# A graph layer on one core: the last tiles are finished an iteration sooner, and the picks are made at the end of a quarter

## The chip, the core and the metric

One NeuronCore of a Trainium2 chip runs the whole kernel as one launch. The time is the device time of one execution in microseconds (us). Before the change it is 906.05 us, the median of three runs (905.99 to 906.22).

## The reference

A layer of message passing over 6250 nodes with 128 features, and 106250 edges sorted by their target. Cut to what matters:

```python
src = x[edge_src]
parts = [relu(x)]
for t in range(3):                       # edge types
    msg = relu(src @ W_e[t].T + b_e[t])
    msg = where(edge_type == t, msg, 0)
    parts.append(segment_sum(msg, edge_dst, 6250))
agg = concatenate(parts, axis=1)         # 6250 x 512
for t in range(3):                       # node types
    updated = where(node_type == t, agg @ W_n[t].T + b_n[t], updated)
out = layernorm(x + (updated + x))
```

All values are fp32. The last 6250 of the edges before sorting are self loops, one for each node.

## The kernel before, in words

**Setup.** TensorE makes a table of all messages (node by edge type, 18750 rows of 128) in device memory. VectorE meanwhile splits the edges into kinds. The last 9050 edges are *early* edges: their source rows are gathered during setup, 36 pairs of chunks. Self loops are taken straight from the table. Up to 128 edges of each of 90 rows, those whose source is among the last 1280 nodes, are *dense*: their source row is picked by a product with a one-hot. What is left of the first 97200 edges is *main*.

**Main stage.** There are 45 iterations j (`NI`) of four quarters g (`NG`), and the code numbers the quarters q = 4j + g. Quarters 0 and 2 hold three chunks of 128 edges, quarters 1 and 3 four. GpSimd gathers a chunk's message rows with one indirect DMA (L753), 14 in an iteration, 630 in all. TensorE sums a group: message rows times a one-hot of their targets (`sum_group`, L1652). GpSimd's gathers for (j+1, g) wait for the sum (j, g) only. VectorE makes the one-hots an iteration ahead (`one_hot`, L1252) and adds the sums into `acc` (L1264) one or two quarters after the iteration's end (`add_sums`).

Around each sum the engines take more steps, each by its own fixed list (`quarter` in each engine's block). TensorE, VectorE, ScalarE and SP wait for each other by semaphores alone, and each runs its list in order. The steps, by where a planner function puts them:

- *Pairs of dense rows* r: `turn_at(r)` is 4r + 3 up to pair 36 and three quarters more for each later one, so 147, 150, 153, ... 171. At that quarter TensorE turns the pair (`dense_turn`, L1673, 20 matmuls), a quarter later VectorE masks it (L1338), three quarters later TensorE makes its messages (`dense_make`, L1686 and L1690), after four it sums them (`dense_sum`, L1698), after five VectorE adds them (`dense_add`). The turn reads one-hots, the *picks* (`dense_onehot`, L1328, two instructions), that VectorE makes at `pick_at(r)`, one quarter after the turn of pair r-1. The picks wait for that turn, since it reads the same tile.
- *Early pairs* go in the same way up to pair 35, with `early_turn`, `early_make` (L1626, L1631), `early_sum`, `early_add`.
- *Tiles* of 128 nodes. Tile t is turned on TensorE at quarter 4(t + 3) (`finish_turn`, L1736). A quarter later its self-loop rows are transposed (`place_selfs`, L1713); after two VectorE adds `acc` and these into a stage (`finish_acc`, L1399); after four TensorE multiplies by the node weights (`finish_linear`, L1747 to L1755); after five VectorE takes the sum with 2x and its statistics (`finish_h`, L1367 to L1375); after six ScalarE takes a root (L917); after seven VectorE writes the row (`finish_y`). The turn of a tile waits for `finish_acc` of the tile before, whose bank it writes; the product waits for `finish_h` of the product before in the same bank, an extra tile's included.
- *Extra tiles*, the last four (45 to 48), whose sums are ready sooner: turned at quarters 69, 97, 133 and 152, multiplied (`LINEAR_AT`) at 74, 102, 138 and 154, their `finish_h` a quarter later.

**Last iteration** (`last_iteration`): tiles 0 to 40 are done in the loop; tiles 41, 42, 43 (sets 2, 0 and 3 of the tiles' buffers) and 44 are finished here. Tiles 42, 43 and 44 have their products behind the last group's sum, 43 and 44 after all additions.

SP loads and stores by its own list: the pairs' rows and types two iterations ahead, tiles in batches of four, stores of finished tiles at the end.

Of the kernel before, what the change touches and what calls it, by code (L numbers as in the profile page):

```python
# [30 lines left out]
ALU = mybir.AluOpType  # L31
# [93 lines left out]
assert sum(n for _, n in BATCHES) == NA and BATCHES[-1] == (SPLIT, TAKEN_LATE)  # L125
# [26 lines left out]
def pick_at(r):  # L152
    return turn_at(r - 1) + 1 if r else NG // 2
# [19 lines left out]

LIMIT_STEP = 15
# [12 lines left out]
LINEAR_AT = [next(q for q in range(at + 2, at + 6) if q % NG == 2) for at in EXTRA_AT]  # L187
# [7 lines left out]


def tile_step(q, later):
    t = (q - later) // NG - (LATE - 1)
    return t if (q - later) % NG == 0 and 0 <= t < SPLIT else None
# [32 lines left out]
def build(nc, x, src, dst, etype, ntype, w_e, b_e, w_n, b_n, out):  # L232
# [6 lines left out]
    with ExitStack() as ctx:  # L239
# [154 lines left out]
        iota_moved = sem("iota_moved")  # L394
        hot_iota_set, acc_zeroed, limits_set = sem("hot_iota_set"), sem("acc_zeroed"), sem("limits_set")
# [101 lines left out]
        def _(sp):  # L497
# [168 lines left out]
            for tile, tiles in BATCHES:  # L666
                if NI <= tile + tiles + LATE and tile + tiles <= SPLIT:
                    sp.wait_ge(fin_y[0], tile + tiles)
                    store_fin(tile, tiles)
            sp.wait_ge(fin_y[2], 1)  # L670
            store_fin(SPLIT)
            sp.wait_ge(fin_y[0], Z0_TILES)
            store_fin(SPLIT + 1)
            sp.wait_ge(ctl_set, 1)
            need = sp.value_load(ctl[0:1, 0:1], min_val=0, max_val=1)
            store_extra(KE)
            sp.wait_ge(fin_y[3], 1)
            store_fin(NA - 1)
            sp.wait_ge(stored[0], 16 * STORES)
# [33 lines left out]
        def _(pool):  # L713
# [13 lines left out]
                      allow_small_or_imprecise_dtypes=True)  # L727
# [54 lines left out]
        def _(act):  # L782
# [136 lines left out]
            def quarter(j, g):  # L919
# [13 lines left out]
                if g == 2 and j > 1:  # L933
                    mask_selfs(j - 2)
# [5 lines left out]
            def last_iteration():  # L940
                finish_x(0, 2, first=True)
                mask_selfs(SPLIT + 1)
                mask_selfs(SPLIT + 2)
                mask_selfs(ORDER[KE])
                finish_x(Z0_TILES - 1)
# [4 lines left out]
                finish_sd(Z0_TILES - 1)  # L950
# [22 lines left out]
        def _(dve):  # L973
# [389 lines left out]
            def finish_h(tile, nth, z=0, slot=None):  # L1363

                x_tile = xg[:, at(tile if slot is None else slot), :].rearrange("p a d -> p (a d)")
                dve.wait_ge(fin_xt[z], nth + 1)
                fin_link(dve.tensor_tensor(h[z][:, :], x_tile, x_tile, ALU.add), nth, z, 1)  # L1367
# [35 lines left out]
            def quarter(j, g, bases_of, pair_base):  # L1403
# [3 lines left out]
                if q in PICKS:  # L1407
                    dense_onehot(PICKS[q])
# [29 lines left out]
                if tile_step(q, ACC_LATER) is not None:  # L1438
# [100 lines left out]
        def _(pe):  # L1539
# [227 lines left out]
            def quarter(j, g):  # L1767
# [12 lines left out]
                if t is not None:  # L1780
                    place_selfs(t, t)
# [100 lines left out]
```

## Time and profile before

| what | value |
|---|---|
| median of three runs | 906.05 us |
| the profiled execution | 907.5 us |
| its span, first to last instruction | 905.7 us |
| busy: TensorE matmul, weight load | 716.2, 598.9 us |
| busy: VectorE, ScalarE, GpSimd | 616.4, 145.0, 673.7 us |
| mean granted TensorE clock | 0.912 of full |

The trace is of one execution. It gives each instruction's start, length, line and tile, the idle time before it, and what ended that idle time. Tiles share memory, so one name can stand for another: `order_f` is the masked pair, `first_wide` and `dense_f` are picks, `work` the one-hots, `emsg` the early masks or the stage of set 2, `src_wide` the dense rows' nodes. "issue" as a releaser means that the profile shows nothing that was waited for.

### The profile page before, as it was taken

Reading aid. Unit: us, or ns where it says so; the run is one execution under the profiler, and the core shown is the slowest. Engines: PE = TensorE matmul, PEld = TensorE weight load, DVE = VectorE, ACT = ScalarE, POOL = GpSimd, SP = SyncE. Lnnn points to the kernel's source line nnn. Section 1 sums busy time; section 2 is a strip of 40 time slices with the busy share of each in tenths; the row PEclk is TensorE's granted clock in tenths of the full one; section 3 lists DMA queues with packets and bytes.
Section 4 is the critical chain, followed back from the end, with each engine's and each line's share of the span. In section 5 each row is a group of like instructions: output and inputs, shape, how many; then the busy total and the mean of one; then the engine's idle time right before and its main releaser. Section 6 shows DMA issues by size and latency. Waiting matters only on the chain.

```text
span 905.7 us, 14050 instructions
## 1 busy us (share of the span) xinstructions
PE 716.2 (79%) x4555; PEld 598.9 (66%) x4555; DVE 616.4 (68%) x1468; ACT 145.0 (16%) x397; POOL 673.7 (74%) x719
## 2 busy tenths in 40 slices
PE   5593056887997988888898878989888798769786
PEld 3362056776876876676687766878767587658674
DVE  7999988476676557557575754775675477656656
ACT  3393000111111101111110120110112011001120
POOL 7777777777777777777777777777777777777772
PEclk9796569998999989999999998999899999989989
DMA  8595533433443343343344342434435334324321
GB/s 245 161 311 147 136 97 76 113 97 50 146 117 105 97 110 107 103 111 92 94 118 116 96 115 78 121 107 111 106 96 114 93 85 118 102 63 128 97 53 45
DMA packets 72065, 101.39 MB, mean 112 GB/s; under 512 B 18137, under 2 KB 55517, under 8 KB 71995
## 3 DMA queue, kind: packets, MB, share of 16 engines
q0 software_dynamic: 22432, 45.99, 21.3%
q1 hardware_dynamic: 46861, 50.45, 18.5%
q10 hardware_dynamic: 2702, 4.08, 1.5%
q8 instruction: 37, 0.61, 0.3%
q14 instruction: 33, 0.27, 0.1%
HBM read 87.47 MB, written 12.97 MB: 111 GB/s over the span
## 4 chain that ended last, share of the span: by engine, by line
POOL 44%; PE 18%; issue 16%; DVE 15%; DMA 6%; SPq 0%; DVEq 0%; POOLq 0%; ACT 0%; ACTq 0%
POOL tab L753 44%; DMA tab<-message_table,idx_t 5%; PE ps L1652 5%; PE ps L1755 3%; PE ps L1673 3%; DVE src_wide L1098 1%; DVE stage L1131 1%; PE ps L1690 1%; PE ps L1686 1%; DVE first_wide L1034 1%; PE ps L1748 1%; DMA dst_raw<-in_dst 1%; PE ps L1631 1%; DVE dst_raw L1091 1%; PE ps L1698 1%
## 5 line engine op out<-in xcount | busy, mean ns | idle before, releaser
L753 POOL DMA_INDIRECT tab<-message_table,idx_t x630 | 595.2, 945 | 194.1 <-issue 185.6
L1652 PE MATMUL ps<-work,tab 128*128 128x126 f32 x1260 | 180.4, 286 | 94.0 <-DMA tab<-message_table,idx_t 68.7
L1252 DVE TENSOR_TENSOR work<-key_t,ps 128x378 f32<-128x378 f32 (+1 forms) x180 | 108.8, 606 | 208.3 <-PE ps L1652 203.7
L1652 PEld LDWEIGHTS ps<-work,tab 128*128 128x128 f32 x1260 | 163.6, 199 | 106.2 <-issue 68.4
L1264 DVE TENSOR_TENSOR acc<-ps,acc 128x126 f32 (+1 forms) x306 | 96.2, 314 | 30.0 <-DVE acc L1264 9.9
L1755 PE MATMUL ps<-wn_t,stage 128*128 128x384 f32 x282 | 104.8, 512 | 0.0
L749 POOL DMA_INDIRECT xg<-in_x,esrc_t x67 | 72.4, 1081 | 20.7 <-issue 16.8
L1755 PEld LDWEIGHTS ps<-wn_t,stage 128*128 128x128 f32 x282 | 56.3, 200 | 40.4 <-issue 5.6
L1673 PE MATMUL ps<-first_wide,tab 128*128 128x128 f32 x450 | 62.8, 291 | 9.5 <-DVE first_wide L1328 6.5
L1673 PEld LDWEIGHTS ps<-first_wide,tab 128*128 128x128 f32 x450 | 58.9, 207 | 9.9 <-issue 9.9
L896 ACT ACTIVATE stage<-ps 128x128 f32<-128x128 f32 x47 | 12.9, 277 | 297.0 <-PE ps L1755 282.1
L1673 PE MATMUL ps<-dense_f,tab 128*128 128x128 f32 x450 | 60.0, 283 | 0.0
L1673 PEld LDWEIGHTS ps<-dense_f,tab 128*128 128x128 f32 x450 | 56.6, 200 | 0.0
L1370 DVE SCALAR_TENSOR_TENSOR h<-ps,mask,h 128x128 f32<-128x128 f32 x147 | 51.6, 351 | 6.7 <-PE ps L1755 1.5
L1626 PE MATMUL ps<-we_t,emsg 128*128 128x128 f32 x216 | 36.3, 312 | 23.0 <-issue 20.4
L917 ACT ACTIVATE sd<-mv,eps 128x1 f32<-128x1 f32 x49 | 14.3, 294 | 230.2 <-DVE mv L1375 230.2
L1626 PEld LDWEIGHTS ps<-we_t,emsg 128*128 128x128 f32 x216 | 32.0, 220 | 27.0 <-issue 23.8
L1686 PE MATMUL ps<-we_t,order_f 128*128 128x128 f32 x270 | 44.1, 308 | 6.5 <-DVE acc L1264 6.5
L1573 PE MATMUL ps<-we_t,work 128*128 128x384 f32 x98 | 44.5, 540 | 3.3 <-DVEq L995 3.2
L1686 PEld LDWEIGHTS ps<-we_t,order_f 128*128 128x128 f32 x270 | 40.7, 225 | 8.1 <-issue 7.8
L1690 PE MATMUL ps<-we_t,order_f 128*128 128x128 f32 x270 | 44.2, 302 | 0.0
L1338 DVE TENSOR_TENSOR order_f<-ps,dst_raw 128x768 f32<-128x768 f32 x45 | 42.7, 949 | 0.1
(260 smaller groups left out, 1021.4 us busy)
## 6 DMA issues: line engine op xcount, KB each, us to landing
tab<-message_table,idx_t POOLq DMA_INDIRECT x630, 2.6
message_table<-tab SPq DMA_DIRECT2D x24, 384.0 KB, 3.5
dst_raw<-dense_types SPq DMA_DIRECT2D x45, 192.0 KB
wn_raw<-message_table SPq DMA_DIRECT2D x22, 384.0 KB, 3.4
src_wide<-dense_lists SPq DMA_DIRECT2D x45, 128.0 KB, 3.2
we_raw<-early_types SPq DMA_DIRECT2D x18, 192.0 KB
be_b<-early_types SPq DMA_DIRECT2D x18, 192.0 KB
work<-in_x ACTq DMA_DIRECT2D x10, 256.0 KB, 5.0
```

The source lines that it names most:

```text
L749: pool.indirect_dma_start(xg[:, q, :], None, x, bass.IndirectOffsetOnAxis(ap=rows, axis=0)).then_inc(x_gathered, 16)
L753: pool.indirect_dma_start(msg[:, slot, :], None, table, bass.IndirectOffsetOnAxis(ap=rows, axis=0)).then_inc(signal, 16)
L1252: dve.tensor_tensor(hot[:, first:first + n, :].rearrange("p c (t w) -> p c t w", w=WIN), keys.broadcast_to((P, n, T, WIN)), iota_win.rearr ...
L1264: dve.tensor_tensor(cols, sums.rearrange("p (t c) -> p t c", t=T), cols, ALU.add).then_inc(added, 1)
L1370: fin_link(dve.scalar_tensor_tensor(h[z][:, :], lin_bank(z, nth)[:, t * D:(t + 1) * D], mask[:, t, at(tile)], h[z][:, :], ALU.mult, ALU.ad ...
L1573: pe.matmul(ps[:, MSG_PS + i, 0:T * D], xt[:, par, i, :], we_t[:, :], start=True, stop=False)
L1626: pe.matmul(early_made[:, 0, :], exm[:, 0, t, :], we_t[:, t * D:(t + 1) * D], start=(t == 0), stop=False)
L1652: ins = pe.matmul(sums_bank(j, g), msg[:, column, :], hot[:, column, :], start=(c == 0), stop=(c == n - 1))
L1673: ins = pe.matmul(dxt_ps[:, :, s * DENSE:(s + 1) * DENSE], dx[:, (SETS - 1 - s) * DT + k, :], donehot[s][:, k, :, :], start=(k == 0), stop ...
L1686: pe.matmul(dmsg_ps[:, 0, :], dxm[:, 0, t, :], we_t[:, t * D:(t + 1) * D], start=(t == 0), stop=False)
L1690: ins = pe.matmul(dmsg_ps[:, 1, :], dxm[:, 1, t, :], we_t[:, t * D:(t + 1) * D], start=False, stop=(t == T - 1))
L1755: ins = pe.matmul(lin, stage[z][:, i, :], wn_t[:, i, :], start=False, stop=(i == T))
```

## The change

1. **Tiles.** A table `TILE_AT` replaces 4(t + 3). Tiles 0 to 32 keep their quarters (12 to 140). Tiles 33 to 36 are turned at 143, 146, 150 and 153, tile 37 at 156, and from there four quarters apart up to tile 41 at 172; before they were at 144, 148, 152, 156 and 160, up to tile 40 at 172. All steps of a tile keep their distance from its turn. In TensorE's quarter the product now stands ahead of the transposes of the self rows.
2. **Extra tiles.** The last product moves from quarter 154 to 156; tile 36's product is at quarter 157.
3. **Picks** move from the start of VectorE's quarter after a pair's turn to the end of the quarter of that turn.
4. **Last iteration.** It finishes tiles 42, 43 and 44 only. Tile 43 has its stage added behind two groups of the last iteration, not behind all additions, and its product ahead of the last group's sum. Only three type products of tile 44 stand behind that sum.
5. **Checks for the general path.** One GpSimd `affine_select` with a wait sets the limit of the last row, so that tile 43 may be finished early.

```diff
-TAKEN_LATE, LATE = 3, 4
+TAKEN_LATE, LATE = 2, 4
 SPLIT = NA - TAKEN_LATE
-Z0_TILES = SPLIT + 1
-STORES = len(BATCHES) - 1 + TAKEN_LATE
+Z0_TILES = SPLIT
+STORES = len(BATCHES) - 1 + BATCHES[-1][1]
...
 def pick_at(r):
-    return turn_at(r - 1) + 1 if r else NG // 2
+    return turn_at(r - 1) if r else NG // 2
...
+def tile_turns():
+    at = []
+    for t in range(SPLIT):
+        if t < LEAD_FROM - LATE + 1:
+            at.append(NG * (t + LATE - 1))
+        else:
+            at.append(max(NG * (t + LATE - 2), turn_at(t + 1) + ADD_LATER - ACC_LATER, at[-1] + NG - 1))
+    return at
...
-LINEAR_AT = [next(q for q in range(at + 2, at + 6) if q % NG == 2) for at in EXTRA_AT]
+LINEAR_AT = [next(q for q in range(at + 2, at + 8)
+                  if (q % NG == 2 or q >= NG * LEAD_FROM) and tile_step(q, LINEAR_LATER) is None
+                  and tile_step(q - 1, LINEAR_LATER) is None) for at in EXTRA_AT]
...
             pool.iota(limit[:, :], pattern=[[P // 2, 2]], base=-P, channel_multiplier=P // 2,
-                      allow_small_or_imprecise_dtypes=True)
+                      allow_small_or_imprecise_dtypes=True).then_inc(limit_made, 1)
+            pool.wait_ge(limit_made, 1)
+            pool.affine_select(out=limit[:, :], in_=limit[:, :], compare_op=ALU.not_equal, fill=float(NA * P),
+                               base=-(HR - 1), pattern=[[0, 2]], channel_multiplier=1)
...
# VectorE, quarter
                 one_hot(j + 1, g)
-                if q in PICKS:
-                    dense_onehot(PICKS[q])
...
+                if q in PICKS:
+                    dense_onehot(PICKS[q])
                 return pair_base
...
# VectorE, last iteration
-                finish_h(SPLIT - 1, SPLIT - 1)
-                dve.wait_ge(group_summed, NG * j + 3)
                 add_sums(j, 0, bases_of[0])
                 add_sums(j, 1, bases_of[1])
-                finish_acc(SPLIT + 1, Z0_TILES - 1, 0, ADDED["main", j, 1])
+                finish_acc(NA - 1, 0, 3, ADDED["main", j, 1])
+                finish_h(SPLIT - 1, SPLIT - 1)
                 finish_h(SPLIT, 0, 2)
+                finish_y(SPLIT - 1, SPLIT - 1)
+                dve.wait_ge(group_summed, NG * j + 3)
                 add_sums(j, 2, bases_of[2])
-                finish_y(SPLIT - 1, SPLIT - 1)
                 finish_y(SPLIT, 0, 2)
+                finish_h(NA - 1, 0, 3)
                 dve.wait_ge(group_summed, NG * j + 4)
                 add_sums(j, 3, bases_of[3])
                 finish_acc(ORDER[KE], KE, 1, ALL_ADDS)
-                finish_acc(NA - 1, 0, 3, ALL_ADDS)
-                finish_h(SPLIT + 1, Z0_TILES - 1)
+                finish_y(NA - 1, 0, 3)
                 finish_h(ORDER[KE], KE, 1, slot=SLOT_OF[KE])
-                finish_y(SPLIT + 1, Z0_TILES - 1)
-                finish_h(NA - 1, 0, 3)
                 finish_y(ORDER[KE], KE, 1, slot=SLOT_OF[KE])
-                finish_y(NA - 1, 0, 3)
...
# TensorE, last iteration
                 finish_linear(SPLIT - 1)
                 sum_group(j, 1)
-                finish_linear(0, 2, first=True)
-                pe.wait_ge(stage_acc[2], 1)
-                finish_turn(SPLIT + 1, Z0_TILES - 1, len(BATCHES))
                 pe.wait_ge(added, ADDED["dense", j, SIDES - 1])
                 finish_turn(NA - 1, 0, len(BATCHES), 3, first=True)
                 pe.wait_ge(fin_var[1], KE)
                 finish_turn(ORDER[KE], KE, NZ, 1)
+                place_selfs(NA - 1, 0, 3)
+                place_selfs(ORDER[KE], KE, 1)
+                finish_linear(0, 2, first=True)
                 pe.wait_ge(added, ADDED["main", j - 1, NG - 1])
                 sum_group(j, 2)
-                place_selfs(SPLIT + 1, Z0_TILES - 1)
-                place_selfs(NA - 1, 0, 3)
-                place_selfs(ORDER[KE], KE, 1)
+                finish_linear(0, 3, first=True)
                 pe.wait_ge(hot_ready, NG * NI)
                 pe.wait_ge(d_hot, NI)
+                linear_open(KE, 1)
                 pe.wait_ge(added, ADDED["main", j, 1])
-                linear_open(KE, 1)
                 sum_group(j, 3)
-                finish_linear(Z0_TILES - 1)
                 linear_types(KE, 1)
-                finish_linear(0, 3, first=True)
```

The masks of the self rows on ScalarE (`mask_selfs`) and SP's stores follow the tiles in the same way.

## Rows read from the trace of the kernel before

**Rows 1.** The page, part 4: the chain that ended last, by engine.

```profile
POOL 44%; PE 18%; issue 16%; DVE 15%; DMA 6%; SPq 0%; DVEq 0%; POOLq 0%; ACT 0%; ACTq 0%
```

**Rows 2.** One line's instructions: count, shortest/median/longest ns, first and last start.

```profile
L753 POOL DMA_INDIRECT tab<-message_table,idx_t x630: 938/944/1047, 101.5 to 889.5; - x158
```

**Rows 3.** Waits of GpSimd: for whom, us in total, times, longest.

```profile
POOL tab L753 <- PE ps L1652: 8.4, 21, 1.1
```

**Rows 4.** Timeline (start, length, engine, line, count, [idle before]): GpSimd, quarters 157 and 158.

```profile
805.58 0.94 POOL L753 DMA_INDIRECT tab<-message_table,idx_t  x1 [0.85 <-PE ps L1652]
...
810.57 0.94 POOL L753 DMA_INDIRECT tab<-message_table,idx_t  x1 [0.30 <-issue]
```

**Rows 5.** Timeline, quarters 145 to 147, TensorE and VectorE.

```profile
750.27 0.91 PE L1626 MATMUL ps<-we_t,emsg 128*128 128x128 f32 x6
...
752.58 0.18 DVE L1375 BATCH_NORM_AGGREGATE mv<-bnst 128x2 f32<-128x6 f32 x1
...
753.11 1.06 PE L1652 MATMUL ps<-work,tab 128*128 128x126 f32 x8
...
754.24 0.55 DVE L1399 TENSOR_TENSOR stage<-acc,ps 128x384 f32<-128x384 f32 x1
```

**Rows 6.** Timeline, VectorE in quarter 157.

```profile
805.35 0.68 DVE L1252 TENSOR_TENSOR work<-key_t,ps 128x504 f32<-128x504 f32 x1 [7.49 <-PE ps L1652]
...
805.94 0.81 DVE L1328 TENSOR_TENSOR first_wide<-src_wide,ps 128x640 f32<-128x640 f32 x1
...
807.41 0.95 DVE L1338 TENSOR_TENSOR order_f<-ps,dst_raw 128x768 f32<-128x768 f32 x1
...
808.89 0.28 DVE L1367 TENSOR_TENSOR h<-xg 128x128 f32<-128x128 f32 x1
...
810.76 0.18 DVE L1375 BATCH_NORM_AGGREGATE mv<-bnst 128x2 f32<-128x6 f32 x1
```

**Rows 7.** Timeline, TensorE in quarters 159 to 163.

```profile
812.89 1.62 PE L1686 MATMUL ps<-we_t,order_f 128*128 128x128 f32 x6 [4.96 <-DVE acc L1264]
...
819.75 0.33 PE L1747 MATMUL ps<-bn_parts,pick_parts 128*128 128x384 bf16 x1
...
822.49 0.90 PE L1698 MATMUL ps<-first_wide,dense_f 128*128 128x216 f32 x4
...
823.22 1.05 PE L1652 MATMUL ps<-work,tab 128*128 128x126 f32 x8
...
824.11 0.49 PE L1713 MATMUL ps<-ident,wn_raw 128*128 128x128 f32 x3
...
824.44 0.83 PE L1652 MATMUL ps<-work,tab 128*128 128x126 f32 x6
...
826.06 0.91 PE L1686 MATMUL ps<-we_t,order_f 128*128 128x128 f32 x6 [0.79 <-DVE acc L1264]
...
827.88 1.28 PE L1673 MATMUL ps<-first_wide,tab 128*128 128x128 f32 x10
...
830.11 1.05 PE L1652 MATMUL ps<-work,tab 128*128 128x126 f32 x8
```

**Rows 8.** Timeline, TensorE in quarters 153 and 156.

```profile
782.77 2.09 PE L1673 MATMUL ps<-first_wide,tab 128*128 128x128 f32 x10 [2.96 <-DVE stage L1399]
...
795.84 0.32 PE L1747 MATMUL ps<-bn_parts,pick_parts 128*128 128x384 bf16 x1 [3.17 <-DVE mv L1375]
...
800.27 0.83 PE L1686 MATMUL ps<-we_t,order_f 128*128 128x128 f32 x6
```

**Rows 9.** Windows: length, PE, PEld, DVE, ACT, POOL busy, clock, DMA, GB/s.

```profile
797.00:800.00 3.00, 3.00 (x6) 1.69 (x5) 0.86 (x2) 0.00 (x0) 2.13 (x3) 0.50 0.18 45
```

**Rows 10.** Timeline of the last iteration, TensorE and VectorE.

```profile
883.36 1.13 PE L1652 MATMUL ps<-work,tab 128*128 128x126 f32 x8 [0.24 <-DMA tab<-message_table,idx_t]
...
892.19 0.49 PE L1652 MATMUL ps<-work,tab 128*128 128x126 f32 x2 [0.31 <-DMA tab<-message_table,idx_t]
...
900.21 1.12 DVE L1370 SCALAR_TENSOR_TENSOR h<-ps,mask,h 128x128 f32<-128x128 f32 x3 [0.36 <-PE ps L1755]
```

More of the change, by code:

```diff
@@ L119 @@
 BATCHES = ([(0, 1)] + [(1 + QUAD * m, QUAD) for m in range(QUADS)] + [(1 + QUAD * QUADS, NA - 1 - QUAD * QUADS)])
-TAKEN_LATE, LATE = 3, 4
+TAKEN_LATE, LATE = 2, 4
 SPLIT = NA - TAKEN_LATE
-Z0_TILES = SPLIT + 1
-STORES = len(BATCHES) - 1 + TAKEN_LATE
+Z0_TILES = SPLIT
+STORES = len(BATCHES) - 1 + BATCHES[-1][1]
 SETS_OF_TILES = 4
-assert sum(n for _, n in BATCHES) == NA and BATCHES[-1] == (SPLIT, TAKEN_LATE)
+assert sum(n for _, n in BATCHES) == NA and BATCHES[-1] == (SPLIT - 1, TAKEN_LATE + 1)
 XB = 4
@@ L171, with tile_step @@
 ACC_LATER, LINEAR_LATER, H_LATER, SD_LATER, Y_LATER = 2, 4, 5, 6, 7
+def tile_turns():
[6 more added lines that the diff above has]
+    return at
+TILE_AT = tile_turns()
+TILES = {at: t for t, at in enumerate(TILE_AT)}
+assert TILE_AT[-1] == NG * (NI - 2)
+def tile_step(q, later):
+    return TILES.get(q - later)
 LIMIT_STEP = 15
@@ L932, in quarter @@
                     dense_relu(dense_step(q, MAKE_LATER))
-                if g == 2 and j > 1:
-                    mask_selfs(j - 2)
+                if tile_step(q, -2) is not None:
+                    mask_selfs(tile_step(q, -2))
+                if q == NG * (NI - 1) - 2:
+                    mask_selfs(SPLIT)
                 if q + 2 in EXTRAS:
@@ L949, in last_iteration @@
                 finish_sd(0, 2)
-                finish_sd(Z0_TILES - 1)
                 finish_sd(0, 3)
@@ L1437, in quarter @@
                     self_masks()
-                if tile_step(q, ACC_LATER) is not None:
-                    finish_acc(tile_step(q, ACC_LATER), tile_step(q, ACC_LATER), 0, ADDED["main", j - 1, NG - 1])
+                t = tile_step(q, ACC_LATER)
+                if t is not None:
+                    finish_acc(t, t, 0, max(ADDED["main", t + 1, NG - 1], ADDED["dense", t + 1, SIDES - 1]))
                 if q - 1 in EXTRAS:
@@ L1785, in quarter @@
                     finish_linear(t, first=t == 0, behind=extras if extras else None)
+                t = tile_step(q, 1)
+                if t is not None:
+                    place_selfs(t, t)
                 if q in EXTRA_LINEAR:
                     n = EXTRA_LINEAR[q]
-                    done = sum(tile_step(before, LINEAR_LATER) is not None for before in range(q))
+                    done = sum(tile_step(before, LINEAR_LATER) is not None for before in range(q + 1))
                     finish_linear(n, 1, first=n == 0, behind=done)
```

23 lines of the change are left out of this document (9 added, 14 removed).

## The prediction

> **What bounds the kernel now.** I read the chain of waits first: GpSimd holds 44% of it, TensorE 18%, VectorE 15% [rows 1]. Then GpSimd's own line. Its 630 gathers of message rows take 0.94 us each and start from 101.5 to 889.5 us [rows 2], so one starts every 788.0 / 629 = 1.253 us, and the 0.30 us between them is issue. GpSimd never rests in the main stage. So the span is three parts: what comes ahead of the first gather, 788 us of gathers with the waits among them, and 905.7 - 890.5 = 15.2 us from the end of the last gather's issue.
>
> Next, where GpSimd waits for TensorE. A gather of iteration j+1, group g overwrites what sum (j, g) reads. I number the quarters q = 4j + g. There are 21 such waits, 8.4 us in all and 1.1 the longest [rows 3]; less the usual 0.30 us each, 2.1 us are lost, I count 2.0. The first that matters is 0.85 us at 805.58 [rows 4]. They come late, where TensorE waits for VectorE: it idles 2.96 us before the pair turn of quarter 153, 3.17 us before the tile product of quarter 156 and 4.96 us before the messages of quarter 159 [rows 7, 8]. Behind the second of these its work runs at the lower of its two clocks (granted 0.50, 1.2 GHz) [rows 9].
>
> **What the change does, part by part.** Three things move: the last tiles, the picks, and the order in the last iteration.
>
> *The last tiles (quarters 143 to 157).* Tiles 33 to 36 are turned at quarters 143, 146, 150 and 153 instead of 144, 148, 152 and 156. The turn of tile t waits until VectorE has added tile t-1's sums (L1399), two quarters after that tile's turn. With four quarters between tiles VectorE has two to do it in; with three it has the quarter just before, where the addition is queued behind nearly all else. TensorE runs its list in order, so the messages, products and the next pair turn all stand behind the waiting turn.
>
> Prices at the full clock, start to start [rows 7]: tile product 822.49 - 819.75 = 2.74; dense sum 0.73; sum of four 0.89; three transposes of the self rows 0.33; pair's messages 827.88 - 826.06 = 1.82; pair turn 830.11 - 827.88 = 2.23. A sum of three lies under that of four, I take 0.67; a lone turn is one of such transposes, 0.11. VectorE's [rows 6]: one-hot 0.59 (I take 0.5 for three chunks), a pair's two picks 807.41 - 805.94 = 1.47, mask and two additions 808.89 - 807.41 = 1.48, of which I give 0.9 to the mask. The first half of a tile's finish (doubling, three products, statistics) runs from 808.89 to 810.76 + 0.18, 2.05 us; the addition for a stage is 0.55 [rows 5]. The dense addition with the register load behind it I estimate at 1.2, twice what is left for the two narrower additions.
>
> After an idle of about 3 us a tile product took 800.27 - 795.84 = 4.43 instead of 2.74 us [rows 8], so a stretch at 1.2 GHz costs up to 1.7. For each long idle I charge 1.0: nearer that end than zero, since a part of the stretch can pass while TensorE still idles. The Trainium skill (TensorE: Matmul & The Clock Gate, HAM oscillation — how this bites in real kernels) states the cost as half of the time spent throttled, and warns of just this pattern, a wait in every round that makes each round start slow. By it each idle would cost 1.7 here, and the trace agrees (1.69).
>
> Now in order of time, on the clock of this trace.
> 1. Quarter 145: tile 32's statistics end at 752.76, and tile 33's addition follows at once: 753.3 (today it is a quarter later, 754.24). Tile 34's turn stands ahead of the messages that start at 750.27 today [rows 5]. New idle of 3.2 us. Then 0.11 + (753.11 - 750.27) 2.84 + 1.0, and quarter 147's sum starts at 757.2 instead of 753.11.
> 2. Quarter 147 now holds tile 33's product and 34's self rows: 0.89 + 2.74 + 0.33 + 2.23 + 0.73 = 6.9, so quarter 148 starts at 764.2. Its pair turn ends at 763.4; from there VectorE needs picks 1.5, one-hot 0.5, dense addition 1.2, mask 0.9, tile 33's statistics 2.1 and tile 34's addition 0.55, until 770.2. Tile 35's turn in quarter 150 waits for it, idle again (some 3.5 us). Then 0.11 + 2.74 + 1.82 + 2.23 + 1.0: quarter 151 starts at 778.1.
> 3. From there picks, one-hot, mask, tile 34's statistics, one-hot, dense addition and tile 35's addition (7.3) end at 785.4. Tile 36's turn in quarter 153 waits for them. This replaces today's wait until 782.77 [rows 8]. Then 0.11 + 1.82 + 1.0 + 2.23: 790.6.
> 4. Quarter 154 (0.67 + 2.74 + 0.33 + 0.73) brings 795.1; sum, one-hot, dense addition, statistics and addition bring 800.5 for tile 36. Tile 37's turn waits for it, in place of the 3.17 us [rows 8]. 0.11 + 2.74 + 1.82 + 2.23 + 1.0: quarter 157 starts at 808.4 (today 804.3, as the one-hot behind its sum starts at 805.35 [rows 6]).
> 5. The extra tile's product moves from quarter 154 to 156, and tile 36's product in 157 shares its bank, so it waits for the extra tile's statistics in VectorE's quarter 157: picks, one-hot, mask, two additions, statistics, 5.7 us, to 814.1. It takes the place of the 4.96 us in quarter 159 [rows 7]. Then 2.74 + 0.33 + 0.73 + 1.0: the sum of quarter 158 starts at 818.9 and ends at 819.7.
>
> The gather that this sum frees starts at 810.57 today, 810.03 without the 0.55 us waited by then [rows 4]. It would start at 820.0, so the waits of GpSimd grow from 2.0 to 10.0 us: **+8 us**. The later quarters need less (about 8.5 in all), so this one decides.
>
> Bounds. If no stretch runs slow the five charges go: +3. At 1.7 each: +11.5. If VectorE is always in time, the waits of today may also vanish: -2.
>
> *The picks.* The two picks (1.47) leave the start of a quarter for the end of the one before, where VectorE waits for the pair turn to end. Sum and one-hot follow that turn at once, so masks come some 0.9 us earlier and no gather with them: GpSimd is never waiting there. Worth 0, apart from what steps 2 to 5 contain. If its cover (VectorE idle at the end of the quarter) is gone, it costs 1.47 at most in the quarters that already stall. SP's row loads keep more than an iteration of lead.
>
> *The affine select at the start* adds a wait and a small instruction to GpSimd before its first gather: 0 to 0.3 us; the fifth gather waits for another engine anyway. I take 0.
>
> *The last iteration.* Two tiles and the extra one are left behind it, not three. From 883.36 [rows 10] TensorE does 0.95 for that sum, turns and self rows with ScalarE between (1.5), tile 42's product 2.74, sum 0.67, tile 43's product 2.74, the opening of tile 44's product 0.65: the last sum starts at 892.6, where the last gather's rows are there at 892.19 today. It ends at 893.7, 1.0 us later than now. Addition, stage addition (1.1) and tile 44's three type products (2.1) give 897.1 for the first instruction of its statistics; today's last tile is there at 900.21 [rows 10], 5.5 us ahead of the end. With one tile left instead of two behind the statistics I take 0.6 less: 902.0 instead of 905.7. **-3.7 us.** Bounds: -4.7 if TensorE is not the later one, -1.5 if a slow stretch falls on the products.
>
> **Sum.** +8.0 - 3.7 = +4.3 on the span of 905.7; the profiled execution took 907.5, 1.8 outside the span, and the median is 1.4 below it. The difference goes on the median: 906.05 + 4.3 = 910.3 us.
>
> **Rivals.**
> - *The lateness is covered.* Only the tail counts. For it: TensorE idles for gathers before the stretch, so at quarter 147 it can be some 7 us later than today unpunished. Against it: the waits follow one another, and each makes the next statistics late. It decides if quarter 158's sum starts before 811 us. Then 906.05 - 3.7 = 902.4, down to 900.3 if today's 2 us go too. Chance 0.17.
> - *Half of it.* No slow stretch after the new idles, GpSimd +3 to +5: 905.4 to 907.4. Chance 0.20.
> - *The rule of the slow stretch in full*, 1.7 for each idle of about 3 us as the products of quarter 156 show [rows 8], and the same again while a wait lasts longer: +11.5 - 3.7 gives 913.9. Chance 0.15. The Trainium skill's page named above is the rule behind it.
> - *The order of the last iteration gives nothing*, as three products in a row delay the last sum: 906.05 + 8 - 1.5 = 912.6. Chance 0.08.
>
> The forecast itself, 907.9 to 912, has 0.40. Faster or slower begins at 0.2% (1.8 us), which is about what can be told from no change. Faster than 904.2: 0.17; within 904.2 to 907.9: 0.20; slower: 0.63. The range 903.5 to 914.0 leaves out the best part of the first rival and the worst of the last two.
>
> **What would show it.** Right: idle of about 3 us before the tile turns (L1736) of quarters 146 and 150, released by VectorE's L1399; one of 4 to 5 us before L1747 in quarter 157, released by the statistics (L1375); clock rows of 0.50 behind them; GpSimd's waits for TensorE some 8 us more; the last gather near 897.5 and 11.5 us from the end of its issue to the span's end. Wrong: the last gather still at 889.5, or TensorE idle only before sums, for gathers.

## The result: slower by 2.0%, and the profile after

The changed kernel takes 924.43 us (median of 4, 922.63 to 925.72); the kernel before took 906.13 us (905.99 to 906.55) beside it. The ratio is 1.020, 95% interval 1.0181 to 1.0218: slower by 18.3 us. I had forecast 910.3 us and at most 914.0, so the direction is right and the size is a quarter of what came.

The profiled execution took 925.72 us. First the page: its span and the chain that ended last, by engine, as in [rows 1]; then the line of GpSimd's waits as in [rows 3].

```profile
span 923.9 us, 14096 instructions
...
POOL 39%; PE 19%; DVE 18%; issue 16%; DMA 6%; DVEq 1%; SPq 0%; ACT 0%; ACTq 0%
```

```profile
POOL tab L773 <- PE ps L1671: 28.2, 21, 7.5
```

GpSimd's part of the chain fell from 44 to 39%, VectorE's rose from 15 to 18%: more of the time is set by work that GpSimd waits for. Those waits are 28.2 us in place of 8.4. By place the longest are these (timeline of GpSimd: start, length, in brackets the idle before it; the usual 0.30 us is in each):

```profile
139.63 0.94 POOL L773 DMA_INDIRECT tab<-message_table,idx_t  x1 [3.12 <-PE ps L1671]
...
769.56 0.94 POOL L773 DMA_INDIRECT tab<-message_table,idx_t  x1 [0.80 <-PE ps L1671]
...
785.40 0.94 POOL L773 DMA_INDIRECT tab<-message_table,idx_t  x1 [3.41 <-PE ps L1671]
...
800.07 0.94 POOL L773 DMA_INDIRECT tab<-message_table,idx_t  x1 [1.24 <-PE ps L1671]
...
805.47 0.94 POOL L773 DMA_INDIRECT tab<-message_table,idx_t  x1 [1.97 <-PE ps L1671]
...
819.65 0.94 POOL L773 DMA_INDIRECT tab<-message_table,idx_t  x1 [5.76 <-PE ps L1671]
...
831.80 0.94 POOL L773 DMA_INDIRECT tab<-message_table,idx_t  x1 [7.46 <-PE ps L1671]
```

The first is for the sum of quarter 4, the others for those of quarters 148, 151, 154, 155, 157 and 158. Less the usual 0.30 us each they are 21.7 us. Behind them TensorE waits where I had said. Its timeline, the rows with an idle of over 3 us and the sums that the walk of the prediction named:

```profile
756.39 0.45 PE L1755 MATMUL ps<-ident,xg 128*128 128x128 f32 x1 [4.43 <-DVE stage L1420]
...
760.82 1.06 PE L1671 MATMUL ps<-work,tab 128*128 128x126 f32 x8
...
768.46 0.83 PE L1671 MATMUL ps<-work,tab 128*128 128x126 f32 x6
...
774.27 0.45 PE L1755 MATMUL ps<-ident,xg 128*128 128x128 f32 x1 [3.19 <-DVE stage L1420]
...
784.07 1.05 PE L1671 MATMUL ps<-work,tab 128*128 128x126 f32 x8
...
792.62 0.45 PE L1755 MATMUL ps<-ident,xg 128*128 128x128 f32 x1 [3.54 <-DVE stage L1420]
...
798.96 0.83 PE L1671 MATMUL ps<-work,tab 128*128 128x126 f32 x6
...
809.68 0.30 PE L1755 MATMUL ps<-ident,xg 128*128 128x128 f32 x1 [3.81 <-DVE stage L1420]
...
818.33 1.06 PE L1671 MATMUL ps<-work,tab 128*128 128x126 f32 x8
...
824.39 0.32 PE L1766 MATMUL ps<-bn_parts,pick_parts 128*128 128x384 bf16 x1 [5.01 <-DVE mv L1396]
...
829.50 0.52 PE L1732 MATMUL ps<-ident,wn_raw 128*128 128x128 f32 x3 [0.52 <-ACT stage L916]
...
830.70 1.50 PE L1671 MATMUL ps<-work,tab 128*128 128x126 f32 x12
```

And the clock in five windows around or just behind these waits, as [rows 9] showed it for one (length, PE busy, granted clock, DMA share, GB/s):

```profile
756.00:760.00 4.00, 3.61 (x16) 0.57 0.23 66
773.00:780.00 7.00, 5.73 (x11) 0.53 0.22 57
790.00:797.00 7.00, 4.38 (x19) 0.53 0.34 107
811.00:815.00 4.00, 4.00 (x12) 0.58 0.21 58
825.00:828.00 3.00, 3.00 (x6) 0.50 0.09 22
```

All five waits are there, and behind each the work runs for part of the way at the lower clock (0.50 is 1.2 GHz): from the end of the wait to the next sum the mean is 0.62, 0.70, 0.63, 0.80 and 0.73. The last iteration, as in [rows 10]: TensorE's wait for a gather, the product that follows at the lower clock, the sum of quarter 177 and the last sum; then GpSimd's last gather.

```profile
899.51 1.46 PE L1671 MATMUL ps<-work,tab 128*128 128x126 f32 x6 [2.60 <-DMA tab<-message_table,idx_t]
...
901.72 1.49 PE L1767 MATMUL ps<-wn_t,stage 128*128 128x384 f32 x2
...
904.99 1.05 PE L1671 MATMUL ps<-work,tab 128*128 128x126 f32 x8
...
914.26 1.05 PE L1671 MATMUL ps<-work,tab 128*128 128x126 f32 x8
```

```profile
909.21 0.94 POOL L773 DMA_INDIRECT tab<-message_table,idx_t  x1 [0.30 <-issue]
```

The last gather's issue ends at 909.21 + 0.94 = 910.15, against 890.48 before, and the span ends 923.9 - 910.15 = 13.75 us later, against 15.2. So 19.7 us came ahead of that point (0.2 of it ahead of the first gather) and 1.5 went behind it.

### The profile page after: what moved, and what is told of

It reads as the page before. It is cut to its first block, busy times and chain, and to the rows that moved or that the text cites. A ratio compares the mean times of both kernels' runs of the same rounds, so it can differ in the third digit from the quotient of the medians.

```text
span 923.9 us, 14096 instructions
## 1 busy us (share of the span) xinstructions
PE 719.6 (78%) x4555; PEld 597.4 (65%) x4555; DVE 618.4 (67%) x1468; ACT 144.9 (16%) x397; POOL 673.7 (73%) x720
## 4 chain that ended last, share of the span: by engine, by line
POOL 39%; PE 19%; DVE 18%; issue 16%; DMA 6%; DVEq 1%; SPq 0%; ACT 0%; ACTq 0%
POOL tab L773 39%; DMA tab<-message_table,idx_t 5%; PE ps L1774 4%; PE ps L1671 4%; PE ps L1692 3%; DVE src_wide L1117 1%; PE ps L1767 1%; DVE stage L1150 1%; DVE h L1391 1%; PE ps L1709 1%; DMA dst_raw<-in_dst 1%; PE ps L1705 1%; DVE first_wide L1053 1%; DVE work L1271 1%; PE ps L1645 1%
## 5 line engine op out<-in xcount | busy, mean ns | idle before, releaser
L1671 PE MATMUL ps<-work,tab 128*128 128x126 f32 x1260 | 182.7, 289 | 102.5 <-DMA tab<-message_table,idx_t 75.6
L1774 PE MATMUL ps<-wn_t,stage 128*128 128x384 f32 x282 | 107.5, 521 | 1.1 <-DVE stage L1420 1.1
L1347 DVE TENSOR_TENSOR first_wide<-src_wide,ps 128x640 f32<-128x640 f32 x45 | 36.9, 820 | 64.3 <-PE ps L1692 63.2
L937 ACT ACTIVATE sd<-mv,eps 128x1 f32<-128x1 f32 x49 | 14.4, 294 | 231.2 <-DVE mv L1396 231.2
L1705 PE MATMUL ps<-we_t,order_f 128*128 128x128 f32 x270 | 41.7, 295 | 3.0 <-DVE acc L1283 3.0
L1709 PE MATMUL ps<-we_t,order_f 128*128 128x128 f32 x270 | 43.6, 300 | 0.0
L932 ACT ACTIVATE wn_raw<-wn_raw,smask 128x128 f32<-128x128 f32 x132 | 42.8, 391 | 0.0
```

The source lines that it names most:

```text
L1671: ins = pe.matmul(sums_bank(j, g), msg[:, column, :], hot[:, column, :], start=(c == 0), stop=(c == n - 1))
L1705: pe.matmul(dmsg_ps[:, 0, :], dxm[:, 0, t, :], we_t[:, t * D:(t + 1) * D], start=(t == 0), stop=False)
L1709: ins = pe.matmul(dmsg_ps[:, 1, :], dxm[:, 1, t, :], we_t[:, t * D:(t + 1) * D], start=False, stop=(t == T - 1))
L1774: ins = pe.matmul(lin, stage[z][:, i, :], wn_t[:, i, :], start=False, stop=(i == T))
```

## The experiments

Each ran beside the kernel before on the same chip; ratios are to that. They ran in four groups. The kernel before had a median of 906.5 us beside kernels 1, 2, 3 and 5, of 906.9 beside 6, 9, 10 and 11, of 908.4 beside 4, 7 and 12, and of 906.6 beside 8, so kernels of different groups are compared by ratio; 0.001 is 0.9 us.

**1. The picks alone** (on the kernel before).

```diff
-    return turn_at(r - 1) + 1 if r else NG // 2
+    return turn_at(r - 1) if r else NG // 2
...
-                if q in PICKS:
-                    dense_onehot(PICKS[q])
...
# at the end of the same quarter
+                if q in PICKS:
+                    dense_onehot(PICKS[q])
```

> The kernel before with the picks alone moved to the end of the quarter before, pair 0's own too (end of quarter 2). Theory: VectorE makes the listing rounds of quarter 2 ahead of pair 0's picks, so the pair turn of quarter 3 and the sum of quarter 4 come some 5.4 us later, one gather waits 2.8 us for that sum near 139.6 us, and nothing makes it up: 906.1 + 2.8 = 908.9 us. The other 43 picks are worth 0. Rival (my prediction as it stands): the picks are worth nothing, 906.1 us. Second rival: the other picks are worth something too, which shows as a time off 908.9 by over 1 us.

Measured 906.86 us (11 runs), ratio 1.0004 (0.9995 to 1.0013). The time is that of my prediction, not of the later theory. The trace shows why: pair 0's turn and the sum of quarter 4 are late as expected (135.87 us, against 133.10), but the gather that waits for that sum still finds its own time. TensorE, then GpSimd:

```profile
131.88 2.48 PE L1673 MATMUL ps<-first_wide,tab 128*128 128x128 f32 x10 [9.13 <-DVE first_wide L1328]
...
135.87 2.40 PE L1652 MATMUL ps<-work,tab 128*128 128x126 f32 x20
```

```profile
136.97 0.94 POOL L753 DMA_INDIRECT tab<-message_table,idx_t  x1 [0.34 <-PE ps L1652]
```

0.04 us above the usual 0.30: the lateness is just used up. In the trace of the changed kernel the first sum of all came 15.7 us behind the first gather, here 13.2, and the 2.5 us between them are nearly all of the wait at 139.63 (2.8 us above the usual). Of the 14 profiled executions of this case, that of before among them, eight have 13.2, four 14.4 to 14.5 and two 15.7. So the move takes away the cover, and as far as these two traces show the execution decides if that costs anything.

**2. The changed kernel with pair 0's picks first.**

```diff
+                if PICKS.get(q) == 0:
+                    dense_onehot(0)
                 if j == 0:
                     list_loops(LISTED // 8 * g // NG, LISTED // 8 * (g + 1) // NG)
...
-                if q in PICKS:
+                if PICKS.get(q):
```

> The changed kernel with pair 0's picks alone put back ahead of the listing rounds of quarter 2. Theory: the 2.81 us wait of the gather at 139.63 us goes, all later waits stay, since those late in the run are set by GpSimd's own pace only up to the wait and each quarter comes 2.8 us sooner: 924.4 - 2.8 = 921.6 us. Rival: the late waits of GpSimd grow by what the early one gives back, as TensorE is the later one there, and the time stays at 924.4 us.

Measured 921.47 us (6 runs), ratio 1.018 (1.0166 to 1.0194). That is where the theory put it, but the interval touches that of the changed kernel, so the gain of about 2 us isn't shown. Much more telling is the profiled execution: it took 913.99 us, the other five 920.14 to 923.16. One program, and 6 us or more between executions. Its waits and its clock in the stage (columns as above) beside those of the changed kernel:

```profile
POOL tab L773 <- PE ps L1673: 20.2, 28, 7.3
...
748.00:782.00 34.00, 26.09 (x171) 0.95 0.38 104
782.00:816.00 34.00, 23.43 (x127) 0.87 0.23 63
```

```profile
748.00:782.00 34.00, 25.34 (x138) 0.85 0.34 93
782.00:816.00 34.00, 25.37 (x148) 0.85 0.30 82
```

The same waits of 3.2, 3.5, 3.8 and 5.0 us for VectorE stand in both. The first, 4.43 us ahead of tile 34's turn, is not in kernel 2's trace: there TensorE had idled 3.53 us for a gather just before. And the work behind the 3.20 us wait of quarter 150 ran at the full clock (1.00 from 767.8 to 774.7 us) and took 6.9 us up to the next sum, while the same work behind the changed kernel's 3.19 us took 9.8 us at a mean of 0.70. No gather waits before 809 us.

**3. and 4. The waits filled** (both on kernel 2). Where TensorE would wait it transposes the identity into a free part of PSUM that nobody reads: 26 times ahead of a tile's turn, 36 times ahead of tile 36's product. The first try filled three of the four turns, all in one bank; the second, shown here, all four, in two.

```diff
             def finish_turn(tile, nth, loads, z=0, first=False):
+                if z == 0 and isinstance(tile, int) and tile in (34, 35, 36, 37):
+                    if tile > 35:
+                        pe.wait_ge(added, ADDED["early", NE - 1, 0])
+                    else:
+                        pe.wait_ge(d_masked, tile + 2)
+                        pe.wait_ge(e_masked, NE)
+                    bank, at_col = (E_MSG_PS, 0) if tile > 35 else (DXT_PS, T * P)
+                    for _ in range(26):
+                        pe.transpose(ps[:, bank, at_col:at_col + P], ident[:, :], ident[:, :])
...
             def linear_open(nth, z=0, first=False, behind=None):
                 lin = lin_bank(z, nth)
+                if z == 0 and tile_of_fill(nth):
+                    for _ in range(36):
+                        pe.transpose(ps[:, E_MSG_PS, 0:P], ident[:, :], ident[:, :])
```

> after_pick0_first with transposes that nobody reads, in a free PSUM bank, where TensorE would wait: 26 ahead of the turns of tiles 35, 36 and 37, 36 ahead of tile 36's product. They add no wait on VectorE. Theory: the half speed behind each wait is what I priced at half; with TensorE kept at work the stretches at granted 0.5 in quarters 150 to 158 go (8.9 us of loss by my count in those four places), and of the 12.6 us that GpSimd waits there for sums 151, 154, 155, 157 and 158 over the usual 0.30 us, 4 to 8 us go: 914 to 918 us. Rival: the clock costs little and the loss is VectorE's lateness handed on from tile to tile; then the time stays within 1 us of after_pick0_first, or rises where the transposes last longer than the wait.

Measured 920.05 us, ratio 1.0158 (1.014 to 1.0177): 2.0 us less than kernel 2 by ratio, so slower than the range expected and near the rival. The trace showed that my own edit spoilt it: in quarter 150 the first unread transpose waited 4.9 us for the last early addition, and the wait for the sum of quarter 151 grew from 3.1 to 6.8 us. The other three quarters were shorter by 1.3 to 1.8 us each.

> after_filled had a flaw: its added wait for the last early addition held the turn of tile 35 for 4.9 us in quarter 150. Here the unread transposes of tiles 34 and 35 go into another free stretch of PSUM, behind a wait that has long been met, so all five waits (turns of quarters 146, 150, 153, 156, product of 157) are filled. Theory: the slow stretches behind them cost what the difference of quarters shows in after_filled (quarter 153 10.94 to 9.68 us, 156 13.30 to 11.49, 157 12.38 to 10.68); with all five filled the sum of quarter 158 comes 8 to 10 us sooner than in the changed kernel for the same start: 921.5 - 9 = 912.5 us, range 910 to 915, near the one execution of after_pick0_first that took 914.0. Rival: the waits for VectorE are 20 us in all and stay, the clock is worth only what after_filled showed, 1.4 us: 918 us or more.

Measured 914.16 us, ratio 1.0063 (1.005 to 1.0076), which is 906.5 x 1.0063 = 912.2 us beside kernel 2: the theory's 912.5. TensorE did more, VectorE the same, and 0.0117 x 906.5 = 10.6 us went. Windows of the filled kernel (length, PE, PEld, DVE, ACT, POOL busy, clock, DMA, GB/s):

```profile
748.00:782.00 34.00, 30.51 (x229) 26.86 (x228) 20.18 (x51) 4.75 (x17) 25.78 (x28) 1.00 0.34 99
782.00:816.00 34.00, 30.09 (x218) 25.73 (x217) 18.44 (x44) 1.71 (x6) 21.40 (x23) 1.00 0.28 82
```

The clock is 1.00 throughout, where it was 0.85. Quarters 146, 150, 153, 156 and 157, each from the start of its sum to that of the next, last 9.69, 13.83, 10.94, 13.30 and 12.38 us in the changed kernel and 8.12, 11.24, 9.80, 11.50 and 10.68 us here: 8.8 us less in all, 1.8 us for each wait.

**5. Two PSUM banks** (on kernel 2): odd tiles from 35 on are turned in the bank of the early messages, which is free by then, so the turn of tile t waits for the addition of tile t-2.

```diff
         def fin_bank(z, nth):
+            if z == 0 and isinstance(nth, int) and nth >= 35 and nth % 2:
+                return E_MSG_PS
...
-                if not first:
+                if z == 0 and isinstance(nth, int) and nth >= 35:
+                    pe.wait_ge(added, ADDED["early", NE - 1, 0])
+                    pe.wait_ge(stage_acc[z], nth - 1)
+                    pe.wait_ge(stage_xt[z], nth)
+                elif not first:
                     pe.wait_ge(stage_acc[z], nth)
```

> after_pick0_first with tiles 35, 37, 39 and 41 turned in another PSUM bank than the even ones, so that the turn of tile t waits for VectorE's addition of tile t-2, no longer of t-1. Theory: the waits of 3 to 4 us ahead of the tile turns of quarters 150, 153 and 156 go, and with them their slow stretches; the one of quarter 146 and the one ahead of tile 36's product in quarter 157 stay. GpSimd's waits of 3.1, 0.9 and 1.7 us for the sums of quarters 151, 154 and 155 go, and those for 157 and 158 fall from 12.6 to some 4: 921.6 - 5.7 - 8 = 908, range 906 to 913 us. Rival: TensorE's lateness is VectorE's load in any order, and the wait moves to the products or messages of the same quarters: within 3 us of after_pick0_first.

Measured 922.41 us, ratio 1.0183 (1.0168 to 1.0199): the rival. The wait that I took off the turns came back two steps on, at the messages and at the products. TensorE:

```profile
789.28 0.91 PE L1709 MATMUL ps<-we_t,order_f 128*128 128x128 f32 x6 [2.71 <-DVE acc L1285]
...
792.86 2.47 PE L1696 MATMUL ps<-first_wide,tab 128*128 128x128 f32 x10 [1.02 <-DVE stage L1422]
...
807.54 0.48 PE L1774 MATMUL ps<-bn_parts,pick_parts 128*128 128x384 bf16 x1 [3.23 <-DVE mv L1398]
```

In quarter 150 my added wait for the early addition stands in place of the old one again (4.85 us), so this run says nothing of that turn.

**6. and 7. The last extra tile's product elsewhere** (on kernel 2), first at quarter 162, then at 166.

```diff
-LINEAR_AT = [next(q for q in range(at + 2, at + 8)
+LINEAR_AT = [166 if at == 152 else next(q for q in range(at + 2, at + 8)
```

> after_pick0_first with the last extra tile's product at quarter 162 instead of 156. Theory (step 5 of the prediction): the product of quarter 156 lengthens that quarter by 2.74 us, and the 5.01 us wait ahead of tile 36's product in quarter 157 is for its statistics; both go, and one slow stretch with them. The gathers freed by sums 157 and 158 wait 12.6 us in the trace of the changed kernel (11.7 us in that of after_pick0_first); 8 to 11 us of it go: 921.5 - 9 = 912 us, range 910 to 914. Rival: VectorE is late by then in any case (the turn of quarter 156 waited for it too), so that the wait moves to the next messages or turn: 917 us or more.

Measured 920.43 us, ratio 1.0153 (1.0139 to 1.0167), 2.4 us less than kernel 2 where 9 were expected: the rival's time. The gathers for quarters 157 and 158 did get their 9.6 us back (12.6 to 3.0), but the product met a new wait in quarter 162, which cost 3.96 and 1.09 us there, and the tail was 16.2 us:

```profile
835.19 0.32 PE L1768 MATMUL ps<-bn_parts,pick_parts 128*128 128x384 bf16 x1 [3.69 <-DVE mv L1396]
```

> extra_product_162 took the waits for the sums of quarters 157 and 158 from 12.6 to 3.0 us, but put the extra product ahead of quarter 163, where it waited 3.69 us for the statistics of tile 37 and cost gathers 3.96 and 1.09 us. At 166 it has two free quarters on either side. Theory: those 5.1 us go, the others stay: 920.4 - 5.1 = 915.3 us, range 913 to 917. Rival: the wait moves on once more (VectorE as such is late): 919 us or more.

Measured 913.55 us, ratio 1.0059 (1.0044 to 1.0074), or 911.9 us beside kernel 2: 11.0 us less than that, and a little under the range expected. GpSimd's waits for TensorE are 15.8 us, none longer than 2.9:

```profile
POOL tab L773 <- PE ps L1673: 15.8, 28, 2.9
```

**8. Both**: 166, and the turns of tiles 34 to 37 filled.

> extra_product_166 with the waits ahead of the turns of tiles 34 to 37 filled with unread transposes, as in after_filled_again (tile 36's product needs no filling, as its wait is gone). Tiles and last iteration stand as in the changed kernel. Theory: the loss of the changed kernel is three things that add up, the early wait from pair 0's picks (gone in both), the slow clock behind the waits, and the extra product ahead of tile 36's. With the last two taken away, of GpSimd's 9.8 us of waits in after_filled_again the 5.5 us for quarter 158 go and most of the 3.7 us for 157, as quarter 156 loses 2.74 us: 1 to 3 us are left, and the tail's gain of some 3 us is seen: ratio to the kernel before 0.996 to 1.000, 903 to 906.5 us. Rival: the placing itself costs (VectorE's addition one quarter ahead of the turn), whatever the clock: no less than 909 us, ratio 1.003.

Measured 908.03 us (12 runs), ratio 1.0014 (1.0002 to 1.0026): between the two theories (1.000 at most, 1.003 at least). 15 of the 16.3 us that kernel 2 loses are gone. 3.0 us of waits are left, the largest 1.5 for the sum of quarter 155, and the tail is 14.3 us. So the placing has a price of its own: kernel 9, placed otherwise and without unread transposes, is some 4 us faster (0.9966).

**9. The tiles spread** (on kernel 2, product at 166): tiles 33 to 37 are turned at 144, 148, 151, 154, 157. Tiles 38 to 41 and the last iteration are those of the changed kernel.

```diff
-            at.append(max(NG * (t + LATE - 2), turn_at(t + 1) + ADD_LATER - ACC_LATER, at[-1] + NG - 1))
+            at.append(max(NG * (t + LATE - 2), NG * 40 - (NG - 1) * (38 - t), at[-1] + NG - 1) if t > 34 else NG * (t + 3))
```

> after_pick0_first with tiles 33 to 37 turned at quarters 144, 148, 151, 154, 157 instead of 143, 146, 150, 153, 156, each a quarter behind a pair turn instead of in the same one, and the last extra product at 166. The last tiles are as early as in the changed kernel. Theory: what costs is the place, a tile turn in the quarter after its predecessor's pair turn, with one quarter of VectorE's list between; here VectorE has the addition of tile t-1 a quarter behind the turn's list too (spacing 3 as before), so the waits ahead of the turns stay at 3 places, shorter by what the pair's picks and mask take (2.4 us each), and those of quarters 146 and 157 go: 908 to 913 us. Rival: VectorE's sum of work in quarters 147 to 160 is what is late, and the place does not matter: within 2 us of extra_product_162. Second rival: all of it fits, only the tail's gain is left: 902 to 905 us.

Measured 903.66 us, ratio 0.9966 (0.9952 to 0.998): faster than both kernels, by 3.1 us than before. The second rival is the one that holds. GpSimd never waits beyond its 0.30 us. First that, then the stage of TensorE with the turns (L1757) of tiles 35, 36 and 37 and the one long wait that is left:

```profile
POOL tab L773 <- PE ps L1673: 6.7, 22, 0.3
```

```profile
769.01 0.30 PE L1757 MATMUL ps<-ident,xg 128*128 128x128 f32 x1
...
783.15 2.45 PE L1694 MATMUL ps<-first_wide,tab 128*128 128x128 f32 x10 [4.01 <-DVE stage L1420]
...
787.75 0.27 PE L1757 MATMUL ps<-ident,xg 128*128 128x128 f32 x1
...
798.80 0.27 PE L1757 MATMUL ps<-ident,xg 128*128 128x128 f32 x1
```

Three quarters between tiles, as in the changed kernel, and no tile's turn waits. Five tiles stand in 13 quarters beside the same pairs in both, so it is the place that counts and not VectorE's load. What about the place is my reading of the two traces: the difference is what TensorE does in the quarter in which VectorE makes the addition. Here that quarter (150, 153, 156) has a pair turn or messages in it and lasts 4.6 to 10.8 us; in the changed kernel the quarters between addition and turn (145; 148 and 149; 152; 155) last 0.9, 0.9 and 0.9, 2.0 and 0.9 us. The long one, 153, contains the 4.01 us wait of the pair turn, and no gather is late for it.

**10. The same with two banks.**

> tiles_spread with the odd tiles from 35 on turned in another PSUM bank, so that no turn waits for the addition of the tile before. Theory: after_two_banks showed the waits move to the products and messages, as VectorE was late; with its list spread by the quarter, the turns' waits that are left are real ones, and 0 to 3 us go against tiles_spread. Rival: nothing, within 0.8 us of tiles_spread.

Measured 903.56 us, ratio 0.996 (0.9946 to 0.9973): no difference, the rival. No tile's turn waited any more, so there was nothing to take.

**11. The changed kernel with all picks in their old place.**

> The changed kernel with all the picks back in their old place, at the head of the quarter behind the pair turn. Only the tiles and the last iteration are then changed. Theory: the picks cost nothing by themselves (picks_alone 906.9 against 906.5), but in quarters 147, 150, 153 and 156 the move puts 1.47 us of them after the tile's addition of the quarter before and none between pair turn and sum; old place: each tile addition behind a pair turn comes at the same time, as VectorE makes them either way before it. So 921.5 us as after_pick0_first, within 1.5. Rival: the move gained time there, as VectorE made the picks while it waited for the turn: 924 to 928 us.

Measured 927.11 us, ratio 1.0239 (1.0216 to 1.0263), 5.3 us above kernel 2: the rival. Five of the six waits behind the late tiles grew, by 0.1 to 1.6 us:

```profile
768.64 0.94 POOL L773 DMA_INDIRECT tab<-message_table,idx_t  x1 [1.89 <-PE ps L1671]
...
800.80 0.94 POOL L773 DMA_INDIRECT tab<-message_table,idx_t  x1 [2.81 <-PE ps L1671]
...
821.34 0.94 POOL L773 DMA_INDIRECT tab<-message_table,idx_t  x1 [6.70 <-PE ps L1671]
```

So the part of the change that I priced at 0 is worth nothing on the kernel before, and some 5 us once the tiles are crowded.

**12. The last sum first** (on kernel 9).

```diff
# TensorE, last iteration
-                linear_open(KE, 1)
                 pe.wait_ge(added, ADDED["main", j, 1])
                 sum_group(j, 3)
+                linear_open(KE, 1)
...
# VectorE, last iteration
-                finish_h(NA - 1, 0, 3)
                 dve.wait_ge(group_summed, NG * j + 4)
                 add_sums(j, 3, bases_of[3])
                 finish_acc(ORDER[KE], KE, 1, ALL_ADDS)
+                finish_h(NA - 1, 0, 3)
```

> tiles_spread with the last sum of TensorE ahead of the opening of the last tile's product, and VectorE's last two additions ahead of tile 43's statistics. In the trace of tiles_spread nothing waits for the last gather: TensorE's list runs without a break from 878 us and the last sum starts at 892.04, some 2 us behind the landing of its rows. Theory: the sum starts 0.8 us sooner, the last tile's stage addition ends at 893.2 instead of 894.1, and tile 43's statistics fill VectorE's wait for the last three products: 903.7 - 0.9 = 902.8 us. Rival: the statistics of tile 43 (1.7 us) then stand ahead of the last tile's and take it back: 903.7 us or more.

Measured 904.98 us, ratio 0.9961 (0.9948 to 0.9974), against 0.9966 for kernel 9. The intervals cover each other: a gain of under 1 us can't be told here. The two traces speak for the rival: the last sum starts 3.4 us behind the one before it in place of 4.2, as expected, but from there the kernel takes 10.6 us to its end in place of 9.7.

## Why the prediction was wrong

**The mechanism held, and four sizes failed.** The forecast was +4.3 us and the measured difference is +18.3. The 14.0 us between are work that the walk left out (5.2), the charge for the slow stretches (3.8), pair 0's picks (2.8) and the tail (2.2), to 0.3 us.

Every wait of steps 1 to 5 came in the quarter, ahead of the operation and for the releaser named: 4.43, 3.19, 3.54, 3.81 and 5.01 us, where I had 3.2 and 3.5 us for the first two and 4 to 5 for the last.

**The charge for the slow stretches was too low by 3.8 us**: "For each long idle I charge 1.0: nearer that end than zero". That is 5.0 us for five waits. Filling the waits gives the price by itself: 8.8 us over five quarters in the traces, 1.8 each, and 10.6 us of the kernel's time. I had the row for 1.7 [rows 8] and took less. The reason that I gave, that part of a stretch passes while TensorE idles, holds for little of it. In the changed kernel the five quarters have mean clocks of 0.82, 0.75, 0.69, 0.87 and 0.86, so half of the time at the lower clock is 12.1 us; counted from the end of each wait alone it is 10.4. Only 1.7 us of it fell on idle time.

The Trainium skill (TensorE: Matmul & The Clock Gate, HAM oscillation — how this bites in real kernels) puts the cost at half of the throttled time. These traces agree in part: 8.8 us lost where the rule gives 12.1, or 10.4 behind the waits.

**The walk left out small waits that repeat.** With the clock at 1.00 (kernel 4) the sum of quarter 158 starts at 819.1 us; my walk without its five charges gives 813.9. Of the 5.2 us between, 2.3 lie between the sums of quarters 151 and 154: the last extra tile is turned in quarter 152 and its addition stands in VectorE's 153, and I had neither in the sum. Three waits of 0.52 us, of the self rows for ScalarE's copy of x (in quarters 147, 154 and 157), are another 1.6 us. The last 1.3 us stay open. ScalarE's copy waits for the product before it, and the diff puts the product directly ahead: a wait that the order made and that I read past.

| sum of quarter | my walk | measured | less the 2.8 us of quarter 4 |
|---|---|---|---|
| 147 | 757.2 | 760.8 | 758.0 |
| 148 | 764.2 | 768.5 | 765.6 |
| 151 | 778.1 | 784.1 | 781.3 |
| 154 | 790.6 | 799.0 | 796.2 |
| 157 | 808.4 | 818.3 | 815.5 |
| 158 | 818.9 | 830.7 | 827.9 |

These 9.0 us and the 2.8 us of quarter 4, with the 8 forecast, are the 19.5 us by which the gathers got longer (808.4 us from the first to the end of the last, before 788.9), to 0.3 us.

**"The picks: worth 0"** was right for the 44 later pairs on the kernel before (kernel 1) and wrong in two ways. Pair 0's picks went behind the listing rounds of quarter 2, which the rows that I chose did not cover: 2.8 us in the trace, where the medians (924.43, and 921.47 with those picks back) don't settle it. And "apart from what steps 2 to 5 contain" hid a gain of some 5 us there (kernel 11).

**The tail**: forecast -3.7 us, in the profiled execution -1.5. I had followed the last gather and asked if TensorE is the later one. It is: from the sum of quarter 177 TensorE's list runs to the end in one piece, and that piece takes 923.9 - 904.99 = 18.9 us (before, 905.7 - 883.36 = 22.3 [rows 10]), whatever the gathers do. Kernels 4 and 7, the same sum in each:

```profile
891.49 1.13 PE L1673 MATMUL ps<-work,tab 128*128 128x126 f32 x8 [0.82 <-DMA tab<-message_table,idx_t]
```

```profile
892.10 1.05 PE L1673 MATMUL ps<-work,tab 128*128 128x126 f32 x8
```

In kernel 4 that sum still waits for its gather, and the tail is 11.9 us, 3.3 less than before; in kernel 7 TensorE comes to it late, 4.1 us ahead of the end of the last issue in place of 7.1, and the tail is 15.1. In the changed kernel it is 5.2 us ahead, behind a product at the lower clock. So the step's size is about right where TensorE arrives in time. It doesn't always: in the twelve executions with a new last iteration (the changed kernel and kernels 2 to 12) the piece takes 18.9 to 19.4 us, but the tail lies between 11.9 and 16.2 us, and four of them gain under 1 us, where my least bound was 1.5. I had given a lost tail 0.08.

**The range** added the bounds of one step at a time. The charges, the tail and the picks went the same way in one execution, and no term stood for what the walk had left out. By the row of 1.7 alone the sum would have been 913.9, the upper edge of my range and still 10.5 us short of the result.

What stays open beside the 1.3 us: why the first sum comes 13.2, 14.4 or 15.7 us behind the first gather.

## What to carry to other kernels

When a step is moved up in a list that engines share, look at how long the *waiting* engine is busy between the producer's step and the waiting one, not at how many steps lie between: three quarters' distance cost nothing where the quarter between was full, and 8.4 us where it was nearly empty (1.0059 against 0.9966, the extra product at 166 in both). That the place made the difference is shown; that it did so by the length of that quarter is read from one pair of traces. Charge each new wait of an engine whose clock falls with its idleness at what the profile shows for such a wait, and give the range the sum of all of them. A wait that can't be removed can be filled with work that nobody reads; here that gave back 10.6 us.

## What the runs showed of the hardware

- One program, two times: kernel 2 took 913.99 us once and 920.1 to 923.2 us five times. The mean granted clock of the whole run was 0.927 in the first and 0.908 to 0.914 in the others. That missing slow stretches are what parts them is likely, not shown, since only the first has a trace.
- A wait of one length can have a slow stretch behind it or none: 1.00 behind 3.20 us of idle (kernel 2, quarter 150), a mean of 0.70 behind 3.19 us (the changed kernel, same quarter and same work).
- Work that nobody reads keeps the clock up: with 140 transposes in the five waits the granted clock was 1.00 over 68 us, against 0.85 in the changed kernel (0.95 and 0.87 in kernel 2's trace). A block of 26 transposes took 3.0 us.
- A PSUM bank beside another for the same purpose gave nothing in two tries (1.0183 against 1.018, 0.996 against 0.9966). In the first an added wait covered one of the three turns that it was for, and in the second no turn waited, so neither shows what a second bank is worth where the turn alone is late.
